# A two-layer decoder on one Trainium2 core: x and the context fetched in transposed layout, and one unit's distance bias written by four transposes

## The reference, cut to what matters

```python
# x, ctx_1024: (32, 128, 128) f32: 32 sequences of 128 tokens, 128 features; H = 16 heads of 8
q = (tokens @ Wq + bq).reshape(B, T, H, dh)
k = (tokens @ Wk + bk).reshape(B, T, H, dh)
v = (tokens @ Wv + bv).reshape(B, T, H, dh)
S = jnp.einsum('bthd,buhd->btuh', q, k)
dist = jnp.abs(pos[None, :] - pos[:, None])
S = S - dist_scale * dist[None, :, :, None]
S = jnp.where(mask_uh[None, None, :, :], -jnp.inf, S)   # head h sees no key u < h
P = jax.nn.softmax(S / sqrt(dh), axis=2)
A = jnp.einsum('btuh,buhd->bthd', P, v).reshape(B, T, D)
x = layernorm(tokens + A @ Wo + bo)                     # then a small FFN, a layer norm ...
# ... a second layer norm, then windowed attention of x to ctx_1024 (keys and values from it)
```

## Time and profile before

| | |
|---|---|
| time of the runs | 1362.21 us, median of 3 (1361.73 to 1365.23) |
| the profiled execution | span 1363.6 us from first to last instruction, mean granted clock 0.964 |
| PE busy | 1199.7 us, 88% |
| DVE busy | 1041.1 us, 76% |
| ACT busy | 863.3 us, 63% |
| POOL busy | 553.3 us, 41% |
| encoder | about 16 to 660 us of the span |
| DMA | 63.54 MB, 47 GB/s in the mean |

### The profile page before, as it was taken

The page is one execution under the profiler, slowest core; times in us unless marked ns, Lnnn a source line. Parts: engine busy times, 40 slices in busy tenths (PEclk is TensorE's granted clock), DMA queues, the critical chain, the costliest instruction groups (busy, mean ns, idle before and its releaser), DMA issues. The chain is left out here.

```text
span 1363.6 us, 31925 instructions
## 1 busy us (share of the span) xinstructions
PE 1199.7 (88%) x10209; PEld 819.7 (60%) x10209; DVE 1041.1 (76%) x3184; ACT 863.3 (63%) x2474; POOL 553.3 (41%) x831
## 2 busy tenths in 40 slices
PE   3789999999999999988489988999999979999796
PEld 2456666666666666654256655555555556777796
DVE  3477888887888888885678867999999975666365
ACT  2677887878887878864246643666666654543464
POOL 1233334425353434432400017556655311556377
PEclk9999999999999999987589988999999999999899
DMA  6100000000000000000122222013100000000673
GB/s 267 52 17 9 17 15 21 29 17 29 15 31 17 26 19 17 13 15 13 53 67 81 82 71 98 24 39 79 43 24 18 5 1 3 17 17 25 178 209 92
DMA packets 71490, 63.54 MB, mean 47 GB/s; under 512 B 10510, under 2 KB 61586, under 8 KB 70688
## 3 DMA queue, kind: packets, MB, share of 16 engines
q1 hardware_dynamic: 62768, 45.27, 11.5%
q0 software_dynamic: 6400, 12.63, 3.0%
q10 hardware_dynamic: 2160, 3.60, 0.8%
HBM read 43.00 MB, written 18.98 MB: 45 GB/s over the span
## 5 line engine op out<-in xcount | busy, mean ns | idle before, releaser
L777 PE MATMUL e_bank_turned<-c_matrices,e_probs 128*128 128x128 f32 x1024 | 166.0, 286 | 16.2 <-ACT e_probs_t L1009 9.0
L703 POOL TENSOR_TENSOR e_rstd<-e_var_eps,c_minus_half 128x1 f32<-128x1 f32 x128 | 71.0, 570 | 253.6 <-DVE e_var_eps L1050 253.3
L1009 ACT ACTIVATE e_probs_t<-e_bank_turned 128x512 f32<-128x512 f32 x256 | 154.9, 605 | 16.0 <-PE e_bank_turned L777 14.5
L1137 DVE TENSOR_REDUCE e_neg_max<-e_bank_scores 128x4 f32<-128x512 f32 x160 | 109.5, 684 | 50.6 <-PE e_bank_scores L820 50.2
L777 PEld LDWEIGHTS e_bank_turned<-c_matrices,e_probs 128*128 128x128 f32 x1024 | 116.7, 145 | 39.9 <-issue 16.1
L787 PE MATMUL e_bank_mix<-e_probs_t,e_values 128*32 128x128 f32 x2048 | 113.2, 294 | 15.5 <-ACT e_probs_t L1009 15.1
L968 ACT ACTIVATE e_probs<-e_scores,e_neg_max 128x128 f32<-128x128 f32 x384 | 123.2, 410 | 1.1 <-DVE e_neg_max L1173 1.1
L1784 ACT ACTIVATE d_probs_t<-d_bank_turned 128x512 f32<-128x512 f32 x128 | 77.4, 605 | 65.9 <-PE d_bank_turned L1661 65.9
L963 ACT ACTIVATE e_probs<-e_scores 128x512 f32<-128x512 f32 x128 | 82.1, 642 | 42.0 <-DVE e_scores L1170 41.4
L706 POOL TENSOR_TENSOR e_k_by_place<-e_q_k_k,c_matrices 128x512 f32<-128x512 f32 x64 | 66.6, 1040 | 102.6 <-DVE e_q_k_k L1181 102.6
L1766 ACT ACTIVATE d_probs<-d_scores 128x512 f32<-128x512 f32 x128 | 80.8, 631 | 38.9 <-DVE d_scores L1807 38.5
(11 more groups left out here) (328 smaller groups left out, 3267.4 us busy)
## 6 DMA issues: line engine op xcount, KB each, us to landing
streamed<-in_s_up SPq DMA_DIRECT2D x36, 258.0 KB, 3.4
sorted_rows<-scratch_sorted SPq DMA_DIRECT2D x72, 64.0 KB, 1.8
scratch_expert_out<-m_y SPq DMA_DIRECT2D x72, 64.0 KB, 1.5
sorted_rows<-scratch_sorted SPq DMA_DIRECT2D x40, 65.0 KB, 3.0
e_x_in<-in_x SPq DMA_DIRECT2D x32, 64.0 KB, 1.9
e_ctx_in<-in_ctx SPq DMA_DIRECT2D x32, 64.0 KB, 2.1
up<-in_m_wgv SPq DMA_DIRECT2D x1, 2048.0 KB, 7.5
up_b<-in_m_bgv SPq DMA_DIRECT2D x1, 2048.0 KB, 14.1
```

What stands on the lines that cost most here:

```text
L777: last = nc.tensor.transpose(turned_bank[:, j * P:(j + 1) * P], pr[k % 3][:, j, :], c["ident"][:])
L1009: nc.scalar.activation(pt[k % 2][:], turned_bank[:], ACT.Copy).then_inc(probs_t_ready, 1)
L1137: nc.vector.tensor_reduce(nmax[k % 4][:], bank, AX.X, ALU.max, negate=True).then_inc(max_ready, 1)
```

## The change

**x and ctx come in transposed as well.** The host lays out `xT` and `ctxT`; x stays as it was, the untransposed context is dropped. SP fetches both transposed tiles straight into `xT_ctxT`: six sequences ahead of everything else, later ones at tick 8n + 29 for sequence n + 6, when PE has last read the tile. The x tile for POOL is fetched on its own at tick 8n - 7. Gone are PE's two transposes (L912, L913), ACT's copy (L996), and SP's store of the transposed context with its waits; the decoder's load reads the host's `ctxT`. The loop begins at tick -8 instead of -11. The experts' weights are issued by SP behind the first projections rather than behind the first transposes.

**The light unit's bias.** DVE makes one more constant, `bias0T`, 128x4x128, the transposed bias of heads 0 to 3, in four instructions before `c_bias0`. `distance` writes the bank by four transposes of it.

```diff
@@ constants
+    c["bias0T"] = sb("bias0T", [P, G, P])
             dve.wait_ge(nds_ready, 1)
+            for j in range(G):
+                nc.vector.tensor_scalar(c["bias0T"][:, j, :], c["dist"][:], c["nds"][:], c["head_col"][:, j:j + 1], ALU.mult, ALU.add)
@@ order of the encoder
-ENCODE_TICKS = range(-11, FRAME * (BATCH + SHIFT) + 64)
+ENCODE_TICKS = range(-8, FRAME * (BATCH + SHIFT) + 64)
-    ("x_x1_mix1", frame_at(tick, -11, 13, 45)), ("hidden", at(tick, 14))) if use[1] is not None])
+    ("x1_mix1", frame_at(tick, 13, 45)), ("hidden", at(tick, 14))) if use[1] is not None])
@@ SP
+            def load_turned(n):
+                if n >= 6:
+                    sp.wait_ge(act_written, ACT_TURNS["q1v1", n - 6] + 1)
+                sp.dma_start(xc[n % 6][:, 0:P], dram_tile(d["xT"], n)).then_inc(xc_loaded[n % 6], 16)
+                sp.dma_start(xc[n % 6][:, P:2 * P], dram_tile(d["ctxT"], n)).then_inc(xc_loaded[n % 6], 16)
             def load(n):
                 if n >= 4:
-                    sp.wait_ge(act_written, ACT_TURNS["x_x1_mix1", n - 6] + 1)
                     sp.wait_ge(x_summed, n - 3)
                 sp.dma_start(xin[n % 4][:], dram_tile(d["x"], n)).then_inc(x_loaded[n % 4], 16)
-                sp.dma_start(cin[n % 4][:], dram_tile(d["ctx"], n)).then_inc(x_loaded[n % 4], 16)
-            for n in range(4):
-                load(n)
-            sp.wait_ge(act_written, ACT_TURNS["x_x1_mix1", -2] + 1)
+            for n in range(6):
+                load_turned(n)
+                if n < 4:
+                    load(n)
+            sp.wait_ge(vec_written, VEC_TURNS["qk_wo1", -1] + 1)
             load_experts(sp, keep, experts0, d, ("m_wgv", "m_wd", "m_bgv", "m_bd"))
             for tick in ENCODE_TICKS:
-                if (n := at(tick, -8)) is not None:
-                    sp.wait_ge(act_read, ACT_TURNS["x_x1_mix1", n - 2] + 1)
-                    sp.dma_start(dram_tile(scr["ctxT"], n), xc[n % 6][:, P:2 * P]).then_inc(ctx_saved[n % 6], 16)
-                    if n + 4 < BATCH:
-                        load(n + 4)
+                if (n := at(tick, -7, BATCH - 4)) is not None:
+                    load(n + 4)
+                if (n := at(tick, 29, BATCH - 6)) is not None:
+                    load_turned(n + 6)
@@ PE
             def distance(k, g):
                 bank_free(k - G + g)
-                nc.tensor.matmul(quad[:, g, :], lhsT=c["ident"][:], rhs=c["bias0"][:, G * g:G * g + G, :].rearrange("p j u -> p (j u)"),
-                                 start=True, stop=False)
+                for j in range(G):
+                    nc.tensor.matmul(quad[:, g, j * P:(j + 1) * P], lhsT=c["bias0T"][:, G * g + j, :], rhs=c["ident"][:],
+                                     start=j == 0, stop=False, is_transpose=True)
...
                     if (n := at(tick, -8)) is not None:
+                        pe.wait_ge(xc_loaded[n % 6], (n // 6) * 32 + 32)
                         last = nc.tensor.matmul(act_bank[:, P:2 * P], lhsT=xc[n % 6][:, 0:P], rhs=c["a_wv"][:], start=True, stop=True)
...
-                    if (n := at(tick, -11)) is not None:
-                        pe.wait_ge(x_loaded[n % 4], (n // 4) * 32 + 32)
-                        nc.tensor.transpose(act_bank[:, 0:P], xin[n % 4][:], c["ident"][:])
-                        last = nc.tensor.transpose(act_bank[:, P:2 * P], cin[n % 4][:], c["ident"][:])
@@ ACT
-                    if (n := at(tick, -10)) is not None:
-                        if n >= 6:
-                            act.wait_ge(ctx_saved[n % 6], n // 6 * 16)
-                        last = nc.scalar.activation(xc[n % 6][:], act_bank[:, 0:2 * P], ACT.Copy)
@@ decoder's load, host's layout
-        sp.dma_start(e["ctxT"][:, part, :], scr["ctxT"][part].rearrange("b p t -> p b t")).then_inc(e["loaded"], 16)
+        sp.dma_start(e["ctxT"][:, part, :], d["ctxT"][part].rearrange("b p t -> p b t")).then_inc(e["loaded"], 16)
-        x=f["x"], ctx=f["ctx_1024"],
+        x=f["x"], xT=con(f["x"].transpose(0, 2, 1)), ctxT=con(f["ctx_1024"].transpose(0, 2, 1)),
+        head_col=np.where(t[:, None] < np.arange(G)[None, :], MASKED, 0.0).astype(np.float32),
```

More of the change, by code:

```diff
@@ L129 @@
     ("a_w1", FF1), ("a_w2", FF1), ("mask_q", G), ("part_iota", 1), ("token", BATCH), ("a_bq", 1), ("a_bk", 1), ("x_bq", 1),
-    ("x_bk", 1), ("a_b1", FF1 // P), ("gate0", EXPERTS), ("gate1", EXPERTS))
+    ("x_bk", 1), ("a_b1", FF1 // P), ("gate0", EXPERTS), ("gate1", EXPERTS), ("head_col", G))
 ROWS = tuple((n, P) for n in ("a_bv", "a_bo", "a_b2", "ln1_g", "ln1_b", "ln2_g", "ln2_b", "x_bv", "x_bo", "l_bo")) + (
@@ L623, in phase_encode @@
         kept = keep["route0"]
-        xin, cin, xc = tiles("x_in", [P, P], 4), tiles("ctx_in", [P, P], 4), tiles("xT_ctxT", [P, 2 * P], 6)
+        xin, xc = tiles("x_in", [P, P], 4), tiles("xT_ctxT", [P, 2 * P], 6)
         x_bo, x_ln2b, x1_b2, x2_bo = (tiles("x_bo", [P, P], 4), tiles("x_ln2b", [P, P], 5), tiles("x1_b2", [P, P], 3),
@@ L640, in phase_encode @@
         bias3 = ctx.enter_context(nc.sbuf_tensor("e_bias3", [P, 3], F32))
-        x_loaded = [sem(f"x_loaded{k}") for k in range(4)]
-        ctx_saved, x3_saved = [sem(f"ctx_saved{k}") for k in range(6)], [sem(f"x3_saved{k}") for k in range(10)]
+        x_loaded, xc_loaded = [sem(f"x_loaded{k}") for k in range(4)], [sem(f"xc_loaded{k}") for k in range(6)]
+        x3_saved = [sem(f"x3_saved{k}") for k in range(10)]
         vec_written, vec_read, act_written, act_read = sem("vec_written"), sem("vec_read"), sem("act_written"), sem("act_read")
@@ L692, in _ @@
                 sp.dma_start(experts0["rows"][k][:], scr["sorted0"][bass.ds(first_rows[k], P), :]).then_inc(experts0["rows_loaded"][k], 16)
-            for k in range(6):
-                sp.wait_ge(ctx_saved[k], 16 * len(range(k, BATCH, 6)))
             for k in range(10):
@@ L727, in _ @@
                 if (n := at(tick, -8)) is not None:
-                    pool.wait_ge(x_loaded[n % 4], (n // 4) * 32 + 32)
+                    pool.wait_ge(x_loaded[n % 4], (n // 4) * 16 + 16)
                     if n == 0:
@@ L843, in _ @@
                     if (n := at(tick, -8)) is not None:
-                        pe.wait_ge(act_read, ACT_TURNS["x_x1_mix1", n - 2] + 1)
                         nc.tensor.matmul(vec_bank[:, 0:P], lhsT=c["a_wq"][:], rhs=xc[n % 6][:, 0:P], start=True, stop=True)
@@ L849, in _ @@
                     if (n := at(tick, 48)) is not None:
-                        pe.wait_ge(act_read, ACT_TURNS["x_x1_mix1", n + 5] + 1)
+                        pe.wait_ge(act_read, ACT_TURNS["x1_mix1", n + 5] + 1)
                         last = nc.tensor.matmul(vec_bank[:, 3 * P:4 * P], lhsT=mixT[1][:], rhs=c["x_wo"][:], start=True, stop=True)
@@ L907, in _ @@
                         .then_inc(act_written, 1)
-                if (f := frame_at(tick, -11, 13, 45)) is not None:
-                    pe.wait_ge(act_read, ACT_TURNS["x_x1_mix1", f])
-                    if (n := at(tick, -11)) is not None:
-                        pe.wait_ge(x_loaded[n % 4], (n // 4) * 32 + 32)
-                        nc.tensor.transpose(act_bank[:, 0:P], xin[n % 4][:], c["ident"][:])
-                        last = nc.tensor.transpose(act_bank[:, P:2 * P], cin[n % 4][:], c["ident"][:])
+                if (f := frame_at(tick, 13, 45)) is not None:
+                    pe.wait_ge(act_read, ACT_TURNS["x1_mix1", f])
                     if (n := at(tick, 13)) is not None:
@@ L988, in _ @@
                         .then_inc(act_read, 1)
-                if (f := frame_at(tick, -10, 14, 46)) is not None:
-                    read("x_x1_mix1", f)
+                if (f := frame_at(tick, 14, 46)) is not None:
+                    read("x1_mix1", f)
                     if (n := at(tick, 14)) is not None:
                         last = nc.scalar.activation(x1T[n % 2][:], act_bank[:, 2 * P:3 * P], ACT.Copy)
-                    if (n := at(tick, -10)) is not None:
-                        if n >= 6:
-                            act.wait_ge(ctx_saved[n % 6], n // 6 * 16)
-                        last = nc.scalar.activation(xc[n % 6][:], act_bank[:, 0:2 * P], ACT.Copy)
                     if at(tick, 46) is not None:
@@ L1061, in scaled @@
                 if n:
-                    dve.wait_ge(act_read, (ACT_TURNS["x_x1_mix1", n + 4] if att else ACT_TURNS["mix0_v0", n]) + 1)
+                    dve.wait_ge(act_read, (ACT_TURNS["x1_mix1", n + 4] if att else ACT_TURNS["mix0_v0", n]) + 1)
                 nc.vector.tensor_tensor(mix[att][:].rearrange("p (h d) -> p h d", d=DH),
@@ L2531, in dram @@
         return nc.dram_tensor("scratch_" + name, shape, F32, kind="Internal").ap()
-    return dict(ctxT=dram("ctxT", (BATCH, P, P)), x3=dram("x3", (BATCH, P, P)),
+    return dict(x3=dram("x3", (BATCH, P, P)),
                 sorted0=dram("sorted0", (EXPERTS * REGION, P)), sorted1=dram("sorted1", (EXPERTS * REGION + P, ROW1)),
```

## The result

The changed kernel takes 1352.15 us (median of 4, 1350.50 to 1352.95) against 1363.61 us for the kernel before in the same comparison (median of 4, 1361.73 to 1365.23). These medians lie 11.5 us apart, but three of the four runs of before are the older ones. The ratio of the comparison is 0.9898, 95% interval 0.9873 to 0.9924: 13.9 us less, where 18.6 were forecast. Applied to the 1362.21 us on which the forecast rests it gives 1348.3, inside the range of 1339 to 1350.5; the plain median is 1.7 above its upper end. Faster was right, and the saving came out a quarter too small.

A forecast was written before the change was run, and what follows sets the result against it. The encoder was taken as bound by PE. Terms 12.7 + 1.3 + 2.2 + 0.7 + 0.4 + 1.3 = 18.6 us saved gave 1345.0 for the span and 1343.6 for the median, range 1339 to 1350.5.

The forecast's parts named there:

- the transposes at 0.49: Light unit's bias on PE: four 128x128 f32 transposes take 0.49 us, like L901, where the wide matmul took 0.96.
- the 0.47 that comes through: Bias in steady frames: PE's 0.47 us saving shortens each frame in full, 27 x 0.47 = 12.7 us.
- Rival 2: Bias transposes on PE run slower, 0.72 us, as weight loads show; half of 12.7 lost, 1350 us; chance 0.11.
- the estimate of 652 ns: Four bias transposes by the skill's rule, 4 x 163 ns with no load hidden; steady frames would save 8.4 us.
- Rival 3: ACT or DVE bounds the frame, PE's savings become waits before L924 and L777; 1358.5 us; chance 0.04.
- Rival 4: Turned tiles come late in SP's queue, L839 waits 1.9 us in 26 sequences; slower, 1393 us; chance 0.04.
- Rival 1: PE's whole saving comes through, also 0.22 us in each of 16 plain frames, 3.5 more; 1340.1 us; chance 0.10.
- The shadow of L1009: Plain frames: the turn L777 starts 0.15 us behind ACT's copy L1009, so removing PE's two transposes (0.22) gives nothing.
- The idle time that I wanted to see named after it: Sign in plain frames: PE idles before the turn, naming L1009, with still 0.15 us from L1009's end.
- the paragraph on DMA: SP's loads: still three 64 KB transfers a sequence; turned tiles land in about 1.9 us, read some 25 us later.
- ACT's copy of the mix, long done: PE's wait at L892, behind the bias: ACT's copy was taken as finished, so it would not hold back the saving.
- only 1 us either way: Allowance for the low-clock stretch moving and the experts' weights arriving later: 1 us either way for both.

The follow-up runs named there:

- the second pair: The changed kernel and the kernel before, each run once more unchanged on one chip: 1354.10 us, ratio 0.9900, and 1368.39 us, ratio 1.0013.

## Why the prediction was right, and where 5 us went

The spans differ by 13.6 us, the sum said 18.6. By its own terms, in the first pair of profiles (of three times 0.22 for the two transposes in early frames, one lies ahead of the third light unit and stands in the first line):

| term of the sum | forecast | measured |
|---|---|---|
| up to the third light unit | 0.4 + 1.3 + 0.22 | 0.75 |
| from there to the sixth | 1.3 + 0.44 | 1.21 |
| 26 steady frames | 12.2 + 2.2 | 12.86 |
| behind the last light unit | 0.5 | -1.2 |

**Right: the transposes at 0.49 and the 0.47 that comes through.** 127.81 to 128.30 is the 0.49 of the earlier trace rows's L901, in a place where they had not run before. Rival 2, transposes slower than those, is out, and with it the estimate of 652 ns, which added the Trainium skill's weight load of 107 ns (TensorE: Matmul & The Clock Gate, section LDWEIGHTS) to its issue gap on my own condition that no load is hidden. In the trace the four, loads included, take 0.49. The kernel with the bias alone shows 0.47 in every plain frame. Rival 3 is out: L927 and the turn behind it wait for nobody, and DVE's wait gave up just what PE gained. Rival 4 is out as well: in the encoder no row of PE waits for a DMA.

**Right: nothing from the two transposes in the plain frames, 0.22 in ten others.** The loads alone leave the plain frame at 18.24 and shorten the frames with logits and with counts by 0.20 to 0.21. Rival 1, the whole of PE's saving, would have made the plain frames 17.55; they are 17.77. The shadow of L1009 was as deep as I had read it. The idle time that I wanted to see named after it does not appear in the row of the turn; the distance of 0.90 alone shows it. With the constants on ACT, where no frame is delayed, the steady part is 468.45. That is 14.4 less than in either profile of before, which is this term of the forecast.

**Too large: the steady frames, by 1.5 in this pair.** 1.0 of it is the delay of L1008, eight times 0.12. The step that failed is the paragraph on DMA. I counted transfers and their landing, found both harmless for the tiles, and took the queue's position as free. What the change had moved was the moment at which SP issues them, into POOL's scatters. ACT's chain, of which I had written that the turn hangs 0.15 behind it, was where it had to show. The other 0.5 lies mostly in two frames (18.72 instead of 18.48, and 17.92 instead of 17.77), which last that long with the loads moved as well. The kernel with the bias alone has both too (18.93 for 18.73, and 17.91 for 17.77), so they are not the loads' work. In each of them DVE sits idle for 0.14 to 0.18 ahead of one instruction (L1136 in the first, L1062 in the second) where it otherwise sits idle for nothing and 0.04. All seven profiles of kernels whose four constants DVE makes have these two, and none of the seven others. They go with DVE's four more instructions, although these are long over by then; by what way is open.

**Too large: the early frames, by 0.5.** The sentence that failed is "ACT's copy of the mix, long done". It holds in the earlier trace rows, not in the early frame, where the units of the second attention do not yet stand between. The changed kernel there:

```profile
62.53 0.33 PE L919 MATMUL e_bank_act<-c_matrices,e_x 128*128 128x128 f32 x1
62.66 0.60 ACT L961 ACTIVATE e_mix_t<-e_bank_mix 128x512 f32<-128x512 f32 x1 [0.55 <-PE e_bank_mix L793]
62.69 0.60 PE L813 MATMUL e_bank_scores<-c_matrices,c_bias0T 128*128 128x128 f32 x4
63.31 0.42 PEld L899 LDWEIGHTS e_bank_vec<-c_matrices,e_mix_t 128*128 128x128 f32 x4 [0.26 <-ACT e_mix_t L961]
63.31 0.66 PE L899 MATMUL e_bank_vec<-c_matrices,e_mix_t 128*128 128x128 f32 x4
```

L961 ends at 63.26 and L899 starts 0.05 behind it, 0.62 after L813 instead of 0.43; the same 0.62 stands at the third light unit, and 0.44 at the fifth. With the bias alone it is 0.44 at the fourth. Both savings lie ahead of the same wait, so they do not add: the bias alone shortens the frame from the 4th to the 5th light unit by 0.35 (13.98 to 13.63), the loads alone by 0.21, both by 0.40, where I had 0.65.

**The start: right for the first light unit by two errors that cancel, wrong behind it.** It comes 0.44 earlier, with 0.4 forecast. The constants cost 1.12, not 0.8 (0.28 each; my bounds were 0.8 to 1.35), and a second pair of transposes that stood right ahead of it went as well, 0.42 (23.53 to 23.95, below), which I had not counted. The first projection, for which I had named 0.4, comes only 0.11 earlier (21.55 for 21.66). Behind it PE's rows of the changed kernel read:

```profile
23.51 1.06 PE L813 MATMUL e_bank_scores<-c_matrices,c_bias0T 128*128 128x128 f32 x4
25.49 2.09 PE L827 MATMUL e_bank_scores<-e_k_by_place,e_q_k_k 32*128 32x512 f32 x8 [0.91 <-POOL e_k_by_place L712]
27.51 0.80 PE L847 MATMUL e_bank_act<-c_matrices,e_xT_ctxT 128*128 128x128 f32 x2
29.57 0.66 PE L783 MATMUL e_bank_turned<-c_matrices,e_probs 128*128 128x128 f32 x4 [0.26 <-ACT e_probs L971]
37.63 1.12 PE L813 MATMUL e_bank_scores<-c_matrices,c_bias0T 128*128 128x128 f32 x4
38.54 0.89 PE L899 MATMUL e_bank_vec<-c_matrices,e_mix_t 128*128 128x128 f32 x4
```

And of the kernel before, from the same place:

```profile
23.53 0.42 PE L912 MATMUL e_bank_act<-c_matrices,e_x_in 128*128 128x128 f32 x1
23.95 1.91 PE L806 MATMUL e_bank_scores<-c_bias,c_matrices 128*128 128x512 f32 x2
25.80 1.15 PE L820 MATMUL e_bank_scores<-e_k_by_place,e_q_k_k 32*128 32x512 f32 x8
26.88 0.49 PE L839 MATMUL e_bank_act<-c_matrices,e_xT_ctxT 128*128 128x128 f32 x2
28.95 0.66 PE L777 MATMUL e_bank_turned<-c_matrices,e_probs 128*128 128x128 f32 x4 [0.91 <-ACT e_probs L968]
```

Before, PE had run without a gap from 21.66 to its scores at 25.80, and these take 1.15, as everywhere at the upper level of 2.4 GHz. In the changed kernel it stands still for 0.91 ahead of L827, and L827 takes 2.09 for the same work, L847 0.80 for 0.49, the lengths of the lower level of 1.2 GHz. (The granted clock is given as 1.00 for this stretch of both traces, so here the level can be read from the lengths alone.) They become short about 28.9, and the first turn comes 0.62 later than before instead of 0.44 earlier. From there on the forecast nearly holds again: L813 to L899 at the lower level is 0.91 against 1.71, 0.80 less for the 0.85 that I had. The gap alone does not keep the clock down. With the constants on POOL PE stands still for the same 0.92 at this place, and the scores behind it take 1.14; in the ten other profiles with the change of the bias they take 2.09, even where the gap is only 0.49 (the bias alone). What decides the level at this point is open, and I had left only 1 us either way for it.

**Behind the encoder** I had counted on nothing but the last 0.5 and lost 1.2. The experts began 20.6 us earlier in the first pair, and the decoder then gave 3.8 back, which the repeats show to be no work of the change. The step from 14.8 us at the last light unit to 20.6 at the experts goes with the clock: this stretch took 108.8 us at a mean granted clock of 0.74 before and 103.0 at 0.81 in the changed kernel, and in the second pair 105.6 at 0.80 before and 108.4 at 0.78. What the other phases behind add, some 3 us more in the changed kernel in the first pair, I did not settle.

## What to carry to other kernels

A row tells what hides a cost in its own kind of frame only: read the frame at the start of the pipeline, and each other kind, before multiplying a saving by their number, and do not add two savings that stand ahead of the same wait. A DMA that is issued in time and lands in time can still cost something by the moment of its issue; list what runs on the other queues at its new place. Before an edit of positions is run, compare the order of the instructions, since a position that passes nobody changes nothing; and before an engine is chosen for work "beside" another, look at what the other has running there: its time alone may not be its time beside it.

## What the runs showed of the hardware that was not expected

- Four f32 tensor_scalar of 128x128 with two per-partition scalars took 1.12 us on DVE, 1.65 on ACT (as one activation each) and 3.81 on POOL, where the first took 2.51 while DVE ran a large instruction and the others 0.44 to 0.45 each.
- Two loads issued by SP between two indirect scatters of POOL came with a delay of 0.10 to 0.14 us before an instruction of ACT, in eight or nine frames of each profile that has them there, on two chips and in the first one of the changed kernel; with the loads 6 us behind not at all, nor in the one profile on another chip whose constants ACT had made. In ACT's rows no wait shows.
- The chips are not alike: on three of them the decoder took 266.5 to 267.6 us from first to last sequence whichever kernel ran, and 263.5 to 263.6 in all three profiles on the fourth, where the kernel before took 1363.18 us against 1366.22 to 1368.90. Kernels from different sets can only be compared by their ratios.
